# Attention with a mixture of experts on one core: experts' rows by transposes back from the turned input, the slot table read in place, weights in pairs, new orders of work

## What is computed

```python
xn = layernorm(x)
# attention: 32 query heads, 16 key/value heads, 64 wide, causal, ALiBi bias
s = softmax(q @ k.T / 8 + slope * (kpos - qpos), causal) @ v @ W_out
# mixture of experts: top 2 of 8 by gate logits, 128 -> 512 -> 128
w = softmax(top2(xn @ gate_w + gate_b))
y = sum_over_2(w * (gelu(xn @ w1[e] + b1[e]) @ w2[e] + b2[e]))
out = x + s * silu(y)
```

## Time and profile before

| | us |
|---|---|
| three runs | 1207.06, 1206.77, 1200.83 |
| their median | 1206.77 |
| the profiled execution, own time | 1205.96 |
| its span, first to last instruction | 1204.2 |

### The profile page before, as it was taken

One profiled execution on the slowest core, in us unless ns is written; L12 is line 12 of the kernel. 1 busy time (PEld: TensorE's weight loads), 2 busy tenths in 40 slices (PEclk: granted clock), 3 DMA queues, 4 the chain that ended last, 5 costly groups with the idle time before them and its releaser, 6 DMA issues.

```text
span 1204.2 us, 48719 instructions
## 1 busy us (share of the span) xinstructions
PE 1111.1 (92%) x16970; PEld 882.0 (73%) x16970; DVE 943.8 (78%) x3099; ACT 948.6 (79%) x1963; POOL 887.0 (74%) x1068
## 2 busy tenths in 40 slices
PE   2689999999999999998999979999999999999996
PEld 1467777777777777776888757777777777777774
DVE  7678778778778888786777668888888888888874
ACT  3568778778778888886666669888888888888884
POOL 6078888888888888887000038899999999998995
PEclk9589999999999999999999999999999999999999
DMA  8525555565566666666435425666555666565552
GB/s 237 193 67 126 125 124 134 127 122 128 119 126 135 131 131 131 125 130 102 90 90 103 98 76 127 131 129 135 129 132 132 133 136 134 132 138 129 134 132 62
DMA packets 272746, 150.96 MB, mean 125 GB/s; under 512 B 177489, under 2 KB 261121, under 8 KB 271873
## 3 DMA queue, kind: packets, MB, share of 16 engines
q1 hardware_dynamic: 268144, 139.32, 53.3%
q0 software_dynamic: 4096, 8.40, 2.7%
q10 hardware_dynamic: 272, 0.13, 0.0%
HBM read 15.76 MB, written 16.78 MB: 27 GB/s over the span
## 4 chain that ended last, share of the span: by engine, by line
PE 72%; DVE 8%; issue 6%; POOL 6%; ACT 3%; DMA 2%; SPq 2%; another core or an unknown queue 0%; ACTq 0%; DVEq 0%; POOLq 0%
PE ps L978 9%; PE ps L1004 9%; PE ps L918 7%; PE ps L920 6%; PE ps L919 6%; PE outs L1036 6%; PE outs L1040 5%; PE ps L1008 5%; PE outs L1038 5%; POOL t_lo L843 5%; PE ps L1005 3%; DVE stage L1613 3%; PE ps L1013 2%; PE ps L987 2%; PE outs L919 1%
## 5 line engine op out<-in xcount | busy, mean ns | idle before, releaser
L843 POOL TENSOR_TENSOR t_lo<-stage 128x512 f16<-128x512 f32 x640 | 657.6, 1040 | 137.9 <-ACT stage L1312 130.1
L1613 DVE CUSTOM_DVE_ANT_0 stage<-ps,kmask 128x512 bf16<-128x512 f32 (+7 forms) x1024 | 425.4, 452 | 146.2 <-PE ps L978 118.3
L1312 ACT ACTIVATE stage<-ps,slope 128x512 f32<-128x512 f32 (+1 forms) x768 | 445.6, 616 | 61.9 <-PE ps L1013 55.4
L1004 PE MATMUL ps<-q_st,k_st 128*128 128x256 f16 (+3 forms) x1024 | 301.0, 301 | 10.5 <-ACT stage L1312 4.8
L1036 PE MATMUL outs<-v_sp,stage 128*128 128x65 f16 x2560 | 275.2, 194 | 14.0 <-DVE stage L1643 5.5
L1040 PE MATMUL outs<-v_sp,t_lo 128*128 128x65 f16 x2560 | 274.9, 193 | 4.8 <-issue 4.8
L1038 PE MATMUL outs<-v_sp,stage 128*128 128x64 f16 x2560 | 274.7, 193 | 4.9 <-issue 4.7
L1036 PEld LDWEIGHTS outs<-v_sp,stage 128*128 128x128 bf16 x2560 | 236.6, 98 | 30.2 <-issue 13.4
L1038 PEld LDWEIGHTS outs<-v_sp,stage 128*128 128x128 bf16 x2560 | 235.2, 98 | 10.9 <-issue 7.0
L1040 PEld LDWEIGHTS outs<-v_sp,t_lo 128*128 128x128 f16 x2560 | 235.1, 98 | 6.4 <-issue 6.4
L1005 PE MATMUL ps<-q_st,k_st 128*128 128x128 f16 x1024 | 223.8, 219 | 0.5 <-issue 0.3
(11 more groups left out here) (222 smaller groups left out, 2722.0 us busy)
## 6 DMA issues: line engine op xcount, KB each, us to landing
q_st<-stage SPq DMA_DIRECT2D x256, 128.0 KB
k_st<-stage SPq DMA_DIRECT2D x128, 128.0 KB
q_st<-stage SPq DMA_DIRECT2D x256, 64.0 KB
k_st<-stage SPq DMA_DIRECT2D x128, 64.0 KB
slot_y<-stage SPq DMA_DIRECT2D x40, 128.0 KB, 2.0
slot_x<-att SPq DMA_DIRECT2D x2, 2048.0 KB, 9.0
wx_raw<-in_L_ffn_w SPq DMA_DIRECT2D x64, 64.0 KB
X<-in_L_attn_inputs SPq DMA_DIRECT2D x4, 512.0 KB, 9.6
```

The costliest lines, as they stand in the source:

```text
L843: pool.tensor_tensor(t_lo[r], t_p[r], upper(t_p[r]), ALU.subtract).then_inc(s[f"lo{u % NG}"], 1)
L1004: pe.matmul(d, k[:, 0, at], q[:, 0, seen], start=(c0 == 0), stop=False, skip_group_check=True)
L1312: e = act.activation(t_p[r][:, c0:c1], S_ps[u % 2][:, c0:c1], ACT.Exp, scale=slope[:, bass.ds(pair_index(n) * 2 * SLOTS + sl * 2 + h, 1)])
L1613: ins = dve.tensor_tensor_reduce(junk[b][:, c0:c0 + w], M_ps[b][:, c0:c0 + w], kmask[:, SEQ - w:SEQ], -1.0 / 1024, 3e38, ALU.add, ALU.min, ...
```

## The change

Five things, each told as what it does.

- `xT_hi` and `xT_lo` become one tensor `xT`, tile by tile, high part beside low part. Eight DMA transposes on SP (`rows_back`, one per batch, of 128x1024 float16) turn it back into `mix`'s memory as rows of high and low parts (`x_rows`). Two are issued before the bodies, the others after task A1 of bodies 0 to 5. ACT's R0 and POOL's subtraction are gone, as is `row_now`.
- `send` and `fetch` take their indices from `slot_of` directly; `slot_now`, I0 and their semaphores are gone. A send waits for its batch's `back` semaphore. There is one semaphore for all sends.
- W0 on SP loads two chunks at once, for every second body, into one of two buffers. These buffers are the memory of the experts' blocks (`xgT`), so SP now also waits for `w_lo` of all 32 chunks before `load(0, 0)`. W0 on POOL has offset -1: chunk n is split in window n+1.
- `ORDER` is new on all engines in both halves. Some tasks come a window earlier (C1 of PE and ACT, M0, Q1).
- The fill of the last 4 expert steps is a table of its own, `FILL`: (task, window from the half's first) to part.

The diff, cut. Of the first table, the order of DVE is left out and of ACT the new one shown; of the second only what PE (new) and POOL do is shown; the new operands of the products and splits of `xT`, and the removed `send_hi`, are left out too:

```diff
         "PE": [
-            ("S0", 0, 0), ("S1", 0, 7), ("P7", -1, 18), ("P8", -1, 23), ("P9", -1, 25), ("C1", 0, 25), ("M0", 1, 29),
-            ("S2", 0, 30), ("S3", 0, 31), ("M1", 1, 33), ("Q1", 1, 33), ("M2", 1, 38), ("V0", 1, 39), ("S4", 0, 40),
-            ("S5", 0, 40), ("P0", 0, 49), ("P1", 0, 52), ("M3", 1, 54), ("S6", 0, 54), ("K0", 2, 55), ("M4", 1, 56),
-            ("P2", 0, 67), ("P3", 0, 68), ("S7", 0, 68), ("M5", 1, 70), ("C0", 1, 70), ("M6", 1, 70), ("P4", 0, 72),
-            ("S8", 0, 72), ("Q0", 2, 73), ("O0", -2, 76), ("M7", 1, 78), ("S9", 0, 86), ("M8", 1, 88), ("P5", 0, 92),
-            ("P6", 0, 93),
+            ("S0", 0, 0), ("S1", 0, 2), ("M1", 1, 4), ("P9", -1, 6), ("M2", 1, 19), ("S2", 0, 19), ("S3", 0, 19),
+            ("K0", 2, 19), ("V0", 1, 19), ("M3", 1, 24), ("M4", 1, 25), ("S4", 0, 29), ("P0", 0, 30), ("M5", 1, 30),
+            ("P1", 0, 31), ("P2", 0, 32), ("S5", 0, 40), ("P3", 0, 40), ("S6", 0, 40), ("C0", 1, 50), ("P4", 0, 57),
+            ("M6", 1, 58), ("S7", 0, 63), ("O0", -2, 69), ("Q0", 2, 72), ("S8", 0, 75), ("S9", 0, 76), ("M7", 1, 76),
+            ("M8", 1, 84), ("Q1", 2, 87), ("P5", 0, 88), ("P6", 0, 91), ("P7", 0, 92), ("C1", 1, 95), ("P8", 0, 98),
+            ("M0", 2, 98),
         ],
...
+            ("D1", 1, 1), ("E0", 0, 4), ("E1", 0, 8), ("E2", 0, 19), ("A1", -1, 20), ("E3", 0, 21), ("K0", 2, 23),
+            ("V0", 1, 34), ("E4", 0, 37), ("E5", 0, 39), ("C0", 1, 54), ("E6", 0, 55), ("E7", 0, 65), ("W0", 1, 70),
+            ("A0", 0, 71), ("Q0", 2, 73), ("E8", 0, 77), ("D0", 2, 79), ("Q1", 2, 82), ("E9", 0, 86), ("C1", 1, 97),
         ],
...
         "POOL": [
-            ("L9", -1, 1), ("L0", 0, 9), ("L1", 0, 10), ("W0", 0, 13), ("L2", 0, 44), ("L3", 0, 48), ("L4", 0, 57),
-            ("D0", 0, 68), ("D1", 0, 85), ("L5", 0, 87), ("L6", 0, 88), ("I0", 1, 91), ("L7", 0, 97), ("L8", 0, 98),
+            ("L8", -1, 2), ("D0", 0, 8), ("L9", -1, 8), ("L0", 0, 10), ("L1", 0, 13), ("L2", 0, 21), ("L3", 0, 26),
+            ("W0", -1, 30), ("L4", 0, 33), ("L5", 0, 57), ("L6", 0, 66), ("L7", 0, 83), ("D1", 0, 97),
         ],
         "SP": [
-            ("C1", 0, 2), ("A0", -1, 8), ("W0", 1, 29), ("A1", -1, 37), ("Q0", 1, 44), ("C0", 1, 65), ("K0", 2, 69),
-            ("Q1", 1, 79), ("K1", 2, 97),
+            ("A0", -1, 8), ("C1", 0, 12), ("Q0", 1, 25), ("Q1", 1, 29), ("K0", 2, 54), ("C0", 1, 64), ("A1", -1, 70),
+            ("W0", 2, 75), ("K1", 2, 87),
         ],
...
+            ("S0", 0, 0), ("C1", 0, 5), ("P8", -1, 11), ("S1", 0, 13), ("P9", -1, 14), ("M0", 1, 14), ("S2", 0, 15),
+            ("M1", 1, 19), ("V0", 1, 20), ("S3", 0, 21), ("S4", 0, 28), ("M2", 1, 28), ("K0", 2, 30), ("M3", 1, 31),
+            ("P0", 0, 34), ("P1", 0, 40), ("M4", 1, 46), ("P2", 0, 48), ("M5", 1, 48), ("S5", 0, 49), ("S6", 0, 49),
+            ("C0", 1, 49), ("P3", 0, 49), ("P4", 0, 49), ("S7", 0, 52), ("M6", 1, 56), ("Q0", 2, 61), ("S8", 0, 62),
+            ("O0", -2, 62), ("S9", 0, 67), ("M7", 1, 77), ("M8", 1, 85), ("Q1", 2, 87), ("P5", 0, 90), ("P6", 0, 91),
+            ("P7", 0, 99),
         ],
...
         "POOL": [
-            ("L0", 0, 9), ("I0", 1, 10), ("L1", 0, 20), ("L2", 0, 24), ("U1", -3, 25), ("L3", 0, 34), ("L4", 0, 35),
-            ("D0", 1, 39), ("L5", 0, 54), ("L6", 0, 59), ("L7", 0, 64), ("D1", 1, 67), ("U2", -3, 79), ("L8", 0, 88),
-            ("G0", 0, 94), ("L9", 0, 94), ("U0", -2, 96),
+            ("L8", -1, 2), ("L9", -1, 5), ("D1", 0, 7), ("G0", -1, 7), ("L0", 0, 10), ("L1", 0, 12), ("L2", 0, 23),
+            ("D0", 1, 40), ("L3", 0, 44), ("L4", 0, 62), ("U2", -3, 65), ("U0", -2, 66), ("L5", 0, 69), ("U1", -2, 74),
+            ("L6", 0, 75), ("L7", 0, 84),
         ],
...
          "SP": ("K0", "K1", "Q0", "Q1"), "POOL": ()}
+
+
+FILL = {
+    "PE": {
+        ("M0", -1): 21, ("M1", -1): 22, ("M2", -1): 23, ("K0", -1): 23, ("M3", -1): 24, ("M4", -1): 25,
+        ("M5", -1): 25, ("C0", -1): 27, ("M6", -1): 27, ("Q0", -1): 27, ("M7", -1): 29, ("M8", -1): 30,
+        ("Q1", -1): 30,
+    },
+    "ACT": {
+        ("D0", -2): 16, ("D1", -1): 23, ("K0", -1): 26, ("C0", -1): 27, ("Q0", -1): 28, ("D0", -1): 28,
+        ("Q1", -1): 30, ("C1", -1): 31,
+    },
+    "DVE": {
+        ("B0", -1): 21, ("B1", -1): 24, ("B2", -1): 25, ("B3", -1): 25, ("B4", -1): 27, ("B5", -1): 27,
+        ("K0", -1): 28, ("B6", -1): 28, ("Q0", -1): 31, ("B7", -1): 31, ("B8", -1): 31, ("Q1", -1): 31,
+    },
+    "POOL": {
+        ("D0", -1): 24,
+    },
+    "SP": {
+        ("C0", -1): 27, ("K0", -1): 28, ("K1", -1): 31,
+    },
+}


...
         g_pair, g_last = piece(11)[:, 0:2 * D], xg_more[:, :].bitcast(F32)
         xgT = [m.rearrange("p (k a q) -> p k a q", k=LOAD * BT, a=2) for m in (piece(11).bitcast(F16), xg_more[:, :])]
+        wx_raw = [m.rearrange("p (k c d) -> p k c d", k=2, c=2) for m in (piece(11), xg_more[:, :].bitcast(F32))]
         y_sb = piece(8).rearrange("p (k t d) -> p k t d", k=2, t=BT)

...
-            for name, off, at in table:
+            for name, off, _ in table:
                 n = w + off
                 if name[0] not in tasks or name == "O0" and n in late or (isinstance(w, int) and not lo <= n < hi):
                     continue
                 if isinstance(w, int) and n == lo and name in AHEAD[engine_name]:
                     continue
-                if part is not None and FILL_AT.get(name, at) * part[1] // 100 != part[0]:
+                if part is not None and FILL[engine_name].get((name, w - lo)) != part:
                     continue
                 tasks[name[0]](n, (phase + off) % UNROLL, int(name[1:]))
                 if "Y" in tasks and isinstance(n, int) and (name, n) in FIRST_ONES[engine_name]:
@@ -335,7 +354,8 @@

-        FIRST_ONES = {"SP": [],
+        BACK = 2
+        FIRST_ONES = {"SP": [("A1", n) for n in range(NB - BACK)],
                       "DVE": [("B0", 0), ("B1", 0), ("B2", 0), ("B3", 0), ("B4", 0), ("B5", 0),
                               ("B6", 1), ("B7", 1), ("B8", 1), ("B0", 2), ("B1", 2), ("B2", 2),
...


             bodies_of_half[:] = lo, hi
-            blocks = (STEPS - FILL_FROM) * STEP * PARTS
             apart = 2
             for i, name in enumerate(AHEAD[engine_name]):
                 if apart * i == b:
                     tasks[name[0]](lo, lo % UNROLL, int(name[1:]))
-            b -= apart * len(AHEAD["PE"])
-            each = (blocks - apart * len(AHEAD["PE"])) // 2
-            if b >= 0:
-                one_window(engine_name, tasks, lo - 2 + b // each, lo, hi, lo + b // each, part=(b % each, each))
+            for w in (lo - 2, lo - 1):
+                one_window(engine_name, tasks, w, lo, hi, w, part=b)

         def block_done(eng, step, j, c):
...
         ZERO_DMAS = -(-ZERO // ZERO_ROW)

         def wx_chunk(w, n):
-            return w[:, bass.ds(n, 1), :, :].rearrange("p g a d -> p (g a d)")
+            return w[:, n, :, :]
+
+        def raw_chunk(n):
+            return wx_raw[n // 2 % 2][:, :, n % 2, :]

         def split_hi(i):

         SENDERS = range(FIRST_SENT, FIRST_SENT + NT - len(TWICE))

-        def sent_with(n, par):
-
-
-            if not isinstance(n, int):
-                return [(n - FIRST_SENT + len(TWICE), par, (n - FIRST_SENT) // UNROLL)]
+        def sent_with(n):
+
             if n not in SENDERS:
                 return []
             t = n - FIRST_SENT + len([b for b in TWICE if b <= n])
-            more = [(t - 1, UNROLL, TWICE.index(n))] if n in TWICE else []
-            return more + [(t, n % UNROLL, (n - FIRST_SENT) // UNROLL)]
+            return [t - 1, t] if n in TWICE else [t]
+
+        x_rows = mix[:, :, :].rearrange("p t d -> p (t d)").bitcast(F16).rearrange("p (t c) -> p t c", c=2 * D)
+
+        def slots(k, t):
+            return bass.IndirectOffsetOnAxis(ap=slot_of[:, k, t:t + 1], axis=0)
+
+        def x_of(q):
+
+            return (xT[:, bass.ds(q * QT, QT), part, :] for part in range(2))
+
+        def by_tile(m):
+            return m.rearrange("p (t c) -> p t c", c=P)

         def x_bank(q):
...
             def load_weights(n, _par, _):

-                need(sp, "w_lo", n)
+                if n % 2:
+                    return
+                need(sp, "w_lo", n - 2)
                 sp.nop(nofuse=True)
-                w1_chunk = w1[bass.ds(n // FC, 1), :, bass.ds(n % FC * P, P)].rearrange("a d f -> d (a f)")
-                w2_chunk = w2_chunks[:, bass.ds(n, 1), :].rearrange("p a d -> p (a d)")
-                for k, w in enumerate((w1_chunk, w2_chunk)):
-                    sp.dma_start(wx_raw[:, k, :], w).then_inc(s["w_in"], 16)
+                to, f = wx_raw[n // 2 % 2], n % FC * P
+                sp.dma_start(to[:, 0, :, :].rearrange("p c d -> p (c d)"), w1[n // FC, :, f:f + 2 * P])\
+                  .then_inc(s["w_in"], 16)
+                sp.dma_start(to[:, 1, :, :], w2_chunks[:, n:n + 2, :]).then_inc(s["w_in"], 16)

```

(81 more changed lines are left out.)

56 lines of the change are left out of this document (21 added, 35 removed), and 30 rows, old and new, of the table ORDER.

## The result

The change made the kernel slower: 1214.47 us, median of five runs (1212.3 to 1216.6), against 1204.93 (1200.83 to 1207.06), ratio 1.0078 with 95% interval [1.0058, 1.0098]. The forecast was 1198. The profiled execution has a span of 1212.7 us against 1204.2.

A forecast was written before the change was run, and what follows sets the result against it. The prediction took back-to-back matmuls on the tensor engine (busy 92%) as the bound, with only idle stretches winnable. Terms summed to -8.8 us on 1205.96, so 1197.2; the median lying 0.8 higher, 1198, range 1184 to 1219.

The forecast's parts named there:

- The scatters: First half, GpSimd: spacing scatters 2.3 us apart removes half the issue stalls, -6.8 us at three places and -4 elsewhere.
- the three places: First-half stretches where a second tile of rows is sent; they cost 13.6 us in all over quiet bodies.
- rival C: First half: all issue stalls go, -13.6-8 instead of -10.8, giving 1187 us; chance 0.16.
- the sign that I gave: Value-split starts in the first half would show no body over 16 us where a second tile is sent.
- Rival A: First half: stalls belong to the scatters however spaced, so the -10.8 falls away, about 1209 us; chance 0.24.
- The shifts: First half: C1 turned a window earlier, so PE's waits for the turned row go, -3 us (0 to -3).
- The prologue: Before body 0's first scores, Q1, C1 and M0 of the next body stand on PE: +1 us (-2 to +4).
- Entry to the experts: First expert matmul 2.4 us late after nearly 4 us without a matmul, then half clock: +5 us (+2 to +8).
- The fill: Last expert blocks: the 1.4 us wait for `q_two` goes, maxima stay in parts 21 to 31; -2 us (-4 to +2).
- The second half: PE idles only 5.7 us there for maxima; new orders win or lose at most some 6 us, taken as 0.
- wrong altogether: The prediction's own failure sign: the second half's mean body time moves by more than 0.2 us.
- Rival B: First half: PE waits for GpSimd's late low parts (L8, L9), 0.5 us in 29 bodies, +14.5, giving 1222 us; chance 0.22.

The follow-up runs named there:

- b4: Kernel before with one edit: GpSimd's first scatter of a first-half body moved ahead, a load between the two scatters; 1193.02 us, ratio 0.9891.
- a0: The changed kernel unaltered, run again where the kernel before takes 1168 to 1170 us; 1191.38 us, ratio 1.018.
- b0: The kernel before, unaltered, profiled where it takes 1168 to 1170 us; ratio 1.0014.
- a3: Changed kernel with the first half's order of the kernel before, on all engines; 1176.97 us, ratio 1.0058.
- a11: The same kernel as a9, run again where the kernel before takes 1205 to 1207 us; 1191.7 us, ratio 0.9889.
- a12: a9 with the changed kernel's own GpSimd list in the first half, its two scatters in different windows; 1178.74 us, ratio 0.9768.
- a7: Changed kernel with VectorE's first-half order from the kernel before; ratio 1.1643.
- a2: Changed kernel with the experts' first load waiting for two fewer weight chunks, the full count waited for only afterwards; 1190.63 us, ratio 1.0163.
- a5: Changed kernel with the fill's maxima up to three parts and rough scores up to one part earlier; 1207.13 us, ratio 1.0009.
- a9: Changed kernel with the first half's order of the kernel before and the fill parts of a5; ratio 0.9973.

## Why the prediction was wrong

**The scatters: right in mechanism, and the size met partly by luck.** Spaced as in b4 they give 11.2 us in the first half's bodies; the two terms were 6.8 and 4. In the three places with a second tile b4 gains 1.8, 2.6 and 2.6 us, 7.0 together, and 4.2 elsewhere. But I had taken half of the stalls to stay, and they went whole, as in rival C; what made it half is the new wait of 8.8 us for the turned row. In the changed kernel the same stalls went (14.4 to 1.0 us of issue at the values), yet the sign that I gave, no body over 16 us at the three places, failed: bodies 5, 7, 10, 12 and 15 take 18.7, 16.9, 17.2, 16.7 and 17.2. Against quiet ones, bodies 5 to 17 lose some 8.5 us where they lost 13.6. Rival A is dead at the long level, and at the short one there is nothing to space.

**The shifts: right.** 3.0 us of waits for the turned row went.

**The step that failed** is one that the sum does not have: the new lists of PE, ScalarE and VectorE in the first half. I priced the moves of GpSimd and SP one by one and took the rest of the first half's new order as free, apart from +1 for the prologue. It cost 15.8 us of waits for the exponentials. The first half's bodies were forecast 12.8 us shorter (-6.8 -4 -3 +1) and came 8.0 longer. PE's idle time did not fall at all, because the 15.8 us stand where the stalls stood; another 8 us came in PE's busy time, and no run takes those apart. PE's list has the third score group at 19 where it stood at 30, and ScalarE's has C1 and D1 ahead of E0. In the timeline above, PE's own work from the end of C1 to that score group takes 2.5 us (426.78 to 429.26), and ScalarE needs 0.46 of it to end the exponential before, then 0.1 + 1.26 + 0.7 for C1's copy, D1 and E0. At the short level this just fits (1.3 us of waits in all in a0); at the long level C1's copy starts 0.46 us later than ScalarE could, and the 0.64 us of wait are mostly that. Even at the short level a0's bodies 2 to 31 take 7.3 us more than b0's. It is not idle time: PE idles 9.1 us in them and 10.4 in b0's, and is busy 436.8 against 428.2. What holds a0's quiet bodies at 15.20 us isn't settled. No row of the kernel before could show this wait; the two new lists side by side could.

**The prologue:** +1 was +5.1 (+5.4 at the short level, a0 against b0). It comes with the first half's order (a3, a11 and a12 don't have it); which list I can't say, since a7, meant to tell, broke the loop instead.

**Entry to the experts: right in mechanism and size.** +5 with a gap of "nearly 4 us": it was 3.54 us and 6.8 us at half clock, +4.3 from the split of body 31 to that of 32. a2 shows the gap to be GpSimd's last chunks; that the half clock goes with it a2 doesn't bear out. The estimate by the Trainium skill (DMA: Bandwidth & Descriptors, the anatomy of one DMA) had the load land in 2.6 us; from issue at 582.17 to the matmul at 585.59 it was 3.4, and the trace's landing was the better guide.

**The fill: wrong sign.** -2 (to +2) was +4.1, and a5 puts its parts at 8.4. I read that the maxima are in parts 21 to 31 "as before" and did not pair them with the scores that need their buffers. By the old rule B1 is in part 22 and M3, which writes the buffer that B1 reads, in 23; in the new table both are in 24 (and M4 in 25 with B2, M5 in 25 with B3). In one part PE must wait until VectorE has come through that block's work, and that is what a0's timeline shows.

**The second half: outside what I held possible** at the long level (0, at most some 6 us; it was -10.3), and there I had said that I would be wrong altogether. The 5.7 us of waits for maxima were only half of it. Between the splits of body 33 and 62 PE's idle time fell from 10.1 to 3.4 us, and its busy time from 430.6 to 427.0: a bound taken from named waits alone was too low. At the short level the same order loses 3.4 us.

Rival B, the one on the other side, came out at the right sign by the wrong way: PE waits 1.4 us for GpSimd's low parts, not 14.5.

## What to carry to other kernels

When the order of work is written out for five engines, a new list must be costed engine against engine: for each wait of the bound engine, add up what its releaser now has in front. One list alone can't be put back to test it; put back all lists of one stage (a3) or one edit (b4, a5). And where a kernel issues indirect DMAs from GpSimd, keep them apart from each other and from the hand-over that the loop hangs on, and time such a change on more than one chip: the same edit was worth 0 us on two of them and 12 on a third. Nor is idle time the whole price of an order: between body 2 and 31 PE's idle time was the same before and after, and the loss of 8 us stood in its busy time.

## What the runs showed of the hardware

**Behind an indirect DMA, what PE signals comes late, at the long level only.** Timeline of the kernel before in the second half, GpSimd's gather, PE's turned shifts, and who waits for PE; then the same place in b0 (short level):
```profile
1019.45 1.01 POOL L837 DMA_INDIRECT y_now<-slot_y,slot_now  x1
...
1019.74 0.22 PE L987 MATMUL ps<-ident,spread 128*128 128x64 f16 x2
...
1021.06 0.20 ACT L1302 CAST turned<-ps 16x64 f16<-16x64 f32 x1 [1.24 <-PE ps L987]
1021.19 0.21 DVE L1649 RECIPROCAL rden<-outs 128x8 f32<-128x8 f32 x1 [1.04 <-PE outs L1040]
```
```profile
990.56 0.22 PE L987 MATMUL ps<-ident,spread 128*128 128x64 f16 x2
990.65 1.01 POOL L837 DMA_INDIRECT y_now<-slot_y,slot_now  x1
990.82 0.20 ACT L1302 CAST turned<-ps 16x64 f16<-16x64 f32 x1 [0.16 <-issue]
```
PE ended at 1019.96 in the one and ScalarE went on 1.10 us later; in the other it took 0.04 us. I counted all copies of turned shifts for which ScalarE stood ready. In the kernel before, second half (760 to 1140 us), 23 of 30 came over 0.2 us late: PE's end lay 0.5 to 1.0 us behind the start of a gather, and the copy began 1.35 to 1.7 us behind that start. In the first half (100 to 500 us) it was 23 of 26, the copies 1.7 to 2.3 us behind the start of the last scatter before them. Of the ten in time, one end lay at a gather's start and nine over 2.9 us behind one. In b0 none of 54 was late, at distances from 0.1 us up. In the changed kernel 23 of 47 were late in the first half (such as the copy shown above at 427.70, 1.59 us behind its scatter; the other 24 lay over 9 us behind one) and none in the second, where PE's ends lie 0.2 us behind a gather or 2.9 and more; in a12, whose scatters too are far from it, none of 53. In b4, where one scatter was moved and nothing else, 18 copies of the first half were late, 1.35 to 1.9 us behind the last scatter. The reading that fits all of this: at the long level a hole of about a microsecond opens behind each indirect DMA. The new order takes PE's turned shifts out of it in the second half and puts them into it in the first, and so the gain of 10 us there and most of the late exponentials here would be its work. That rests on places and times and on the two levels; no run moves a gather alone.

The issue stalls fit this (holes that touch, two scatters 1.3 us apart, last long enough to stop PE itself): in the 20 bodies of the kernel before with two scatters and one stall, PE went on 1.45 to 1.95 us behind the start of the second. But that is argued, not shown. Open is what the two levels are, and how an indirect DMA gets in the way of the signals.

The two levels differ by 35 us in the kernel before, 23 in the change, 28 in a9 and a11. The median low part takes 1039 ns in the kernel before and in b0, the median exponential 682 in both (100 to 500 us), so the difference isn't in these instructions.
